# Strided attention after an expert layer: where two context pieces are loaded and when all four are multiplied

## The reference, cut to what matters

```python
Q = (hidden_states @ Wq.T + bq).reshape(B, Tq, H, D).transpose(0, 2, 1, 3)
K = (key_value_states @ Wk.T + bk).reshape(B, Tk, H, D).transpose(0, 2, 1, 3)
V = (key_value_states @ Wv.T + bv).reshape(B, Tk, H, D).transpose(0, 2, 1, 3)
m = Tk // stride
idx = jnp.arange(H)[:, None] + stride * jnp.arange(m)[None, :]
...
scores = jnp.einsum('bhqd,bhkd->bhqk', Q, Kg) * scaling
attn = jax.nn.softmax(scores, axis=-1)
out = jnp.einsum('bhqk,bhkd->bhqd', attn, Vg)
```

## Time and profile before

| what | value |
|---|---|
| median of three runs | 2059.59 us (2058.01 to 2061.52) |
| the profiled execution, its own time | 2049.21 us |
| its span, first to last instruction | 2047.5 us |
| mean granted clock of TensorE | 0.964 of full speed |
| TensorE busy | 1892.9 us, 92% |
| VectorE, ScalarE, GpSimd busy | 51%, 39%, 31% |
| queue q1 (hardware), q0 (software) | 30.6%, 2.4% of 16 engines' span |

### The profile page before, as it was taken

How to read it: one execution, slowest core, us unless ns; L and a number is a source line. 1 busy time by engine, 2 the same in 40 slices (tenths; PEclk the granted TensorE clock), 3 DMA queues, 4 the chain that set the end, 5 groups by cost and what they waited for, 6 DMA issues and landing times. The chain is left out here.

```text
span 2047.5 us, 35305 instructions
## 1 busy us (share of the span) xinstructions
PE 1892.9 (92%) x12136; PEld 1542.4 (75%) x12136; DVE 1043.0 (51%) x2405; ACT 801.4 (39%) x1728; POOL 641.8 (31%) x522
## 2 busy tenths in 40 slices
PE   5799999999999999999589999999997876999994
PEld 3588788787878787878468888888875656999983
DVE  5616465565656565645553333233335755554564
ACT  3324243333434343433343334233313534555650
POOL 1220110302020202000045554355520204787872
PEclk9899999999999999999789999999998977999997
DMA  8730213122121112010333333133368034545546
GB/s 289 237 104 30 75 38 72 46 60 58 54 63 54 30 54 59 9 26 10 105 119 109 113 113 123 54 105 110 116 210 283 13 129 136 182 163 165 204 150 207
DMA packets 131587, 218.85 MB, mean 107 GB/s; under 512 B 46075, under 2 KB 50971, under 8 KB 130671
## 3 DMA queue, kind: packets, MB, share of 16 engines
q1 hardware_dynamic: 126431, 200.46, 30.6%
q0 software_dynamic: 5008, 16.48, 2.4%
HBM read 188.87 MB, written 28.04 MB: 106 GB/s over the span
## 5 line engine op out<-in xcount | busy, mean ns | idle before, releaser
L492 POOL TENSOR_TENSOR a_cols<-a_cols,a_moments_b 128x722 f32<-128x722 f32 x32 | 56.6, 1768 | 545.3 <-DMA a_moments_b<-a_moments_dram 545.3
L634 PE MATMUL a_kv_ps<-a_kvin_hi,a_wk_hi 128*128 128x512 f32 (+1 forms) x512 | 195.5, 382 | 0.0
L1098 PE MATMUL f_banks<-f_wab_hi,f_x_hi 128*128 x448 | 183.6, 410 | 2.6 <-DVE f_x_lo L1785 1.4
L635 PE MATMUL a_kv_ps<-a_kvin_lo,a_wk_hi 128*128 128x512 f32 (+1 forms) x512 | 179.7, 351 | 0.0
L636 PE MATMUL a_kv_ps<-a_kvin_hi,a_wk_lo 128*128 128x512 f32 (+1 forms) x512 | 179.6, 351 | 0.0
L1100 PE MATMUL f_banks<-f_wab_hi,f_x_lo 128*128 x448 | 176.3, 394 | 0.0
L1099 PE MATMUL f_banks<-f_wab_lo,f_x_hi 128*128 x448 | 175.8, 392 | 0.0
L568 ACT ACTIVATE a_probs<-a_probs,a_neg_max 100x822 f32<-100x822 f32 x128 | 125.9, 984 | 115.1 <-DVE a_neg_max L916 115.1
L1807 DVE TENSOR_TENSOR f_h_sb<-f_h_sb,f_banks 128x256 f32<-128x256 f32 x112 | 47.2, 421 | 239.9 <-ACT f_h_sb L1530 237.6
L634 PE MATMUL a_kv_ps<-a_wv_hi,a_kvin_hi 128*128 128x512 f32 (+1 forms) x384 | 157.0, 409 | 2.3 <-DVE a_k_lo L909 2.2
L1530 ACT ACTIVATE f_h_sb<-f_banks 128x256 f32<-128x256 f32 x112 | 43.1, 385 | 292.8 <-PE f_banks L1100 283.9
(11 more groups left out here) (419 smaller groups left out, 4786.1 us busy)
## 6 DMA issues: line engine op xcount, KB each, us to landing
f_raw<-f_pieces SPq DMA_DIRECT2D x94, 256.0 KB, 2.7
m_raw<-m_pieces SPq DMA_DIRECT2D x92, 256.0 KB, 2.9
f_wab_raw<-f_pieces SPq DMA_DIRECT2D x42, 512.0 KB, 5.9
m_wab_raw<-m_pieces SPq DMA_DIRECT2D x42, 512.0 KB, 6.0
a_cols<-ctx_cols SPq DMA_DIRECT2D x8, 1444.0 KB, 7.5
a_rows<-ctx SPq DMA_DIRECT2D x8, 1280.0 KB
ahead_piece<-g_ctx SPq DMA_DIRECT2D x2, 2880.0 KB, 20.7
a_moments_b<-a_moments_dram SPq DMA_DIRECT2D x7, 722.0 KB
```

Source lines behind the costliest of these rows:

```text
L634: nc.tensor.matmul(out, hi_l, hi_r, start=first, stop=False)
L635: nc.tensor.matmul(out, hi_l, lo_r, start=False, stop=False)
L1098: nc.tensor.matmul(out, left_hi, right_hi, start=start, stop=False)
```

## The change

In the expert layer SyncE loads context pieces 1 and 2 directly behind the x rows, in both branches. In the attention they are no longer issued. TensorE multiplies pieces 0, 1 and 2 first, then turns tokens 0 to 3, then multiplies piece 3, and only then starts the queries; `half(0)`, `tokens` 4 to 7 and `half(1)` follow with nothing between them and the scores. The use of the four banks and ScalarE's program follow that order.

```diff
--- before.py
+++ after.py
@@ -1398,6 +1398,8 @@
                     ahead.load_values(sp)
                     ahead.load_piece(sp, 0)
                     handed.load_stream(sp)
+                    ahead.load_piece(sp, 1)
+                    ahead.load_piece(sp, 2)
                 else:
                     sp.wait_ge(y_scattered, 16 * SLOTS)
             with sp.Else():
@@ -2083,9 +2087,9 @@
         ROUTED = 3
         GROUPS = ((0, 1, 2, 3), (4, 5), (6, 7))
         bank_use = {}
-        for kind, n in (("k", 0), ("v", 0), *(("x", b) for b in range(HB)), ("k", 1), ("v", 1), *(("q", m) for m in range(KD)),
-                        ("k", 2), ("v", 2), *(("x", b) for b in range(HB, B)), *(("q", m) for m in range(KD, 2 * KD)),
-                        ("k", 3), ("v", 3)):
+        for kind, n in (*((kind, c) for c in range(3) for kind in "kv"), *(("x", b) for b in range(HB)),
+                        ("k", 3), ("v", 3), *(("q", m) for m in range(KD)),
+                        *(("x", b) for b in range(HB, B)), *(("q", m) for m in range(KD, 2 * KD))):
             bank_use[kind, n] = len(bank_use)
         BANK_USES = len(bank_use) // 4
         assert len(bank_use) % 4 == 0
@@ -2107,10 +2111,8 @@
             sp.wait_ge(sums.tail_done, 1)
             sp.wait_ge(sums.scattered, 16 * sums.core)
             sums.load_half(sp, 0)
-            ahead.load_piece(sp, 1)
             sp.dma_start(wq_raw[:, :, :], wq_t).then_inc(wq_loaded, 16)
             sums.load_half(sp, 1)
-            ahead.load_piece(sp, 2)
             ahead.load_piece(sp, 3)
             sp.wait_ge(mid_done, B)
             sp.dma_start(wo_raw[:, :, :], wo_t).then_inc(wo_loaded, 16)
@@ -2181,24 +2183,26 @@
                                      scale=SCALE).then_inc(fill_free("q", n), 1)
 
             act.wait_ge(zero_k, 1)
+            act.wait_ge(const_done, 2)
             move_keys(0)
             move_values(0)
-            act.wait_ge(const_done, 2)
-            for g in range(2):
-                deviations(g)
-                for b in EQUAL[g]:
-                    move_tokens(b)
+            move_keys(1)
+            deviations(0)
+            move_values(1)
+            move_keys(2)
+            deviations(1)
+            move_values(2)
+            for b in range(HB):
+                move_tokens(b)
             act.wait_ge(wq_loaded, 16)
             for k in range(KD):
                 nc.scalar.activation(wq_hi[:, k, :], wq_raw[:, k, :], ACT.Copy).then_inc(wq_hi_done, 1)
-            move_keys(1)
-            move_values(1)
             act.wait_ge(q_bias_done, 1)
+            move_keys(3)
+            move_values(3)
             for n in range(KD):
                 move_queries(n)
             deviations(2)
-            move_keys(2)
-            move_values(2)
             for b in range(HB, B):
                 move_tokens(b)
             def high_output_weights(k):
@@ -2210,8 +2214,6 @@
                 move_queries(n)
                 if n >= KD + 2:
                     high_output_weights(n - KD - 2)
-            move_keys(3)
-            move_values(3)
             for k in range(2, KD):
                 high_output_weights(k)
             act.wait_ge(c_loaded, 32)
@@ -2310,18 +2312,17 @@
                 for n in range(KD * h, KD * h + KD):
                     queries(n)
 
-            context(0)
+            for c in range(3):
+                context(c)
             pe.wait_ge(const_done, 3)
             for b in range(HB):
                 tokens(b)
-            context(1)
+            context(3)
             pe.wait_ge(wq_lo_done, KD)
             half(0)
-            context(2)
             for b in range(HB, B):
                 tokens(b)
             half(1)
-            context(3)
 
             def element(b):
                 if b >= 4:
```

## The result

The changed kernel takes 2068.79 us in the median of six runs (2067.74 to 2073.19), the kernel before 2057.71 us in six (2052.99 to 2061.52): 11.1 us more, a ratio of 1.0065 with a 95% interval of 1.0047 to 1.0082. (The ratio is worked out beside the difference of the medians and can come out a little apart from it; its interval means 9.7 to 16.9 us.) The forecast was 2072 us and +12.4 us.

A forecast was written before the change was run, and what follows sets the result against it. From 1536 until piece 3 lands, transfers bound the stretch as much as TensorE. Queries 22.0 us later less a 9.6 us gain gave +12.4 us: 2061.6 us profiled, plus 10.4 us for the median, 2072 us; range 2062 to 2077.5.

The forecast's parts named there:

- Room for the pieces: Pieces 1 and 2 behind the x rows: 4.8 us of room for 14.1 us of transfers; SyncE goes on 11.0 us later.
- no or few packets of the software queue while pieces move: Sign expected in the changed profile, from 1520 to about 1540, with the scatters kept behind the pieces.
- Landing of piece 3: Later loads on q1: piece 3 lands at 1575.2, only 3 us earlier than before; 1573.5 at the earliest.
- The bias: Load queued behind the pieces, landing between 1540 and 1546; costs nothing, as tokens 0 to 3 come at 1559.
- `context(3)` ahead of the queries: TensorE waits for piece 3 until 1575.2, then multiplies for 7.0 us; queries start at 1582.2, 22.0 us later.
- Gain behind the queries' start: From queries to softmax 28.9 us instead of 38.45: a gain of 9.6 us, bounds 8 and 11.1.
- Sum: Whole kernel: 22.0 - 9.6 = +12.4 us, 2061.6 us profiled, 2072 us median; bounds +7 and +17.
- Rival (a): Extra loads cost the scatters nothing; piece 3 lands at 1567.4, +2.6 to +4.6 us, 2062 to 2064; chance 0.12.
- Rival (b): Row loads of `y` speed up, piece 3 8.4 us earlier: alone +4 us, with (a) -5 us, 2055; chance 0.12.
- A shift of 1598.65 should be the shift of the whole kernel: The softmax starts at 1598.65; from there the work is one chain into the second expert layer.

The follow-up runs named there:

- e1: Changed kernel with `context(3)` moved back behind the queries, early loads of pieces 1 and 2 kept; +3.6 us against before, ratio 1.0026.
- e9: Changed kernel with 64 transposes of the identity between `tokens(3)` and `context(3)`, where TensorE waits; +11.7 us against before, ratio 1.0051.
- e8: As e1, but pieces 1 and 2 are not loaded and their products read piece 0; -4.4 us against before, ratio 0.9970.
- e6: Kernel before with wq issued ahead of piece 1, `context(1)` behind the queries' first half, tokens 4 to 7 ahead of `context(2)`; -0.7 us, ratio 0.9996.
- e10: e6 with 56 transposes behind `context(0)` and 28 between `tokens(3)` and the queries' first half; -1.8 us against before, ratio 0.9988.
- e5: Kernel before with only piece 1 issued early and `context(1)` right behind `context(0)`; +2.9 us against before, ratio 1.0008.

## Why the prediction was right, point by point

- **Room for the pieces.** Right in kind: the early pieces are paid for by what stands behind them. The step that failed is the software queue's share: the forecast let the scatters be last, behind both pieces. The rows after show them kept out only while x rows move; with the pieces both queues send packets in equal numbers. So the scatters were through at +28.4, before piece 2 (+32.4), and SyncE went on 9.1 us late, not 11.0; the sign "no or few packets of the software queue while pieces move" failed. It changed little behind it: the rows of `y` are queued on q1 behind piece 2, and the first combine, forecast at +34.3, came at +34.6, 11.2 us late. The Trainium skill (DMA: Bandwidth & Descriptors, Queues, rings and completion order) had taking turns between queues, which I had put at 1 to 2 us lower; the trace agrees, against my reading of the earlier trace rows, for pieces and scatters. How many packets one turn has, the counts don't show.
- **Landing of piece 3.** Worked out at +58.5 (1575.2 less 1516.74), measured +57.8, 3.7 us earlier than before where 3 were worked out. The estimate from the sum of the bytes needs no order. Its limit of 4.8 us, beyond which "no order of the same bytes can gain more", was too firm, though: in e1, with the same loads, piece 3 lands 5.2 us earlier than before.
- **The bias.** Named as queued behind the pieces and hidden. It came later than the 1540 to 1546 I gave: ScalarE waited for it until 1554.40, or +32.7, and TensorE 3.9 us for the first moved keys before `context(2)`. That product ended at 1564.8, just as the first rows were normalised, so it still cost nothing, but with no slack left.
- **`context(3)` ahead of the queries.** The wait was 10.2 us, the product 6.8 us for 7.0, its cause, the clock, shown by e9. The queries started at +64.6 for +65.5. e1, which moves this product back and takes 6.9 of the 11.5 us away, shows that this is the larger part of the loss.
- **Gain behind the queries' start.** From there to the softmax 28.8 us (1615.09 - 1586.33) for 28.9.
- **Sum.** +11.5 us in the stage for +12.4, +11.1 us in the medians. The 0.9 us is about what the earlier landing gives. The upper bound is added up wrongly: 22.0, 2 to 3 us for the scatters, 2.9 for a `context(3)` of 9.9 instead of 7.0, less 8 make +19 to +20, not +17. The forecast for the profiled execution, 2061.6 us, missed (2068.85); the 10.4 us added to get to the median belonged to that one profile before, since after, profile and median are 0.1 us apart. For the median they cancel out, so it rests on the +12.4 alone.
- **Rival (a)**, scatters unharmed: out, 9.1 us. **Rival (b)**, row loads faster afterwards: out. From SyncE's going on to piece 3's landing there are 29.3 us in the changed kernel, where 28.0 were worked out and the rival needs 19.6; in e8, with neither piece 1 nor 2 anywhere, there are still 27.3 us. (The rates that the rival starts from, 1.64 MB in 9.3 and in 8.0 us, are 42% and 49% of the pieces' 0.42 MB per us, not half to two thirds.)
- **"A shift of 1598.65 should be the shift of the whole kernel".** This holds for the medians within about 2 us: in all eleven kernels the shift of the softmax and that of the median lie at most 2.0 us apart. It doesn't hold for one profile. From the softmax to the second expert layer's `m_rows_at` it is 97.6 us before and 100.7 us after. The busy tables of both around the second attention group show a lower clock in the one than in the other, with about the same work (112 and 109 matmuls):

```profile
1647.00:1659.00 12.00, 11.50 (x112) 9.76 (x112) 4.18 (x10) 4.84 (x12) 0.00 (x0) 0.87 0.30 98
```

```profile
1663.00:1678.00 15.00, 14.01 (x109) 11.68 (x109) 4.62 (x11) 4.92 (x12) 0.00 (x0) 0.69 0.26 83
```

The first is before, the second after. Over all profiles this later stretch took from 97.6 to 103.9 us, with no relation to the medians (e6 103.9 and -0.7 us). With 4.95 us ahead of the stage this makes up the rest of the 19.6 us between the two spans.

## What to carry to other kernels

A load that is issued early isn't free because the engine that needs it is idle: ask how much room the DMA engines have until the next thing that somebody waits for, and count everything that then lands behind it, a small bias and another queue's scatters too. An in-order engine must not take first the product whose data lands last; 5 us of work put ahead of ready queries brought a wait of 10.2 us and 1.8 us of cold clock, and cost 6.9 us net (changed kernel against e1). And idle time that a faster chain opens on TensorE comes back in part as a lower clock on what follows, so a product that nobody waits for is best kept right ahead of the one that everybody does: e10, which fills the idle time and keeps `context(2)` ahead of the second half, has the softmax 3.0 us earlier in its profile, though its time can't be told from before.

## What the runs showed of the hardware

Two queues with work sent packets in equal numbers: 780 of one and 776 of the other in 17 us, which with 5.6 and 3.3 KB each on average (4.33 and 2.58 MB) gave them 62% and 39% of the engines' time. In e5 it was 411 and 409 in 9 us. Alternating packet by packet would do that, but so would equal turns of several packets. While rows of 2048 bytes from the x tensor were on the way, the software queue had no packet for 7 us in one profile and 5 in the other, though a scatter was issued at 1524.28 in the one and at 1519.33 in the other. Not all of that is being kept out, since a scatter's packets start late anyway: those of the fourth, issued at 1519.90 in the changed kernel, began between 1521.0 and 1521.5. Why the x rows keep the software queue out and the pieces don't is open. Pieces and scatters together moved 0.41 MB per us (4.33 + 2.58 MB in 17 us), the x rows 0.22 (1.57 MB in 7 us) at the same full engines.
